# GpSimd scatters the results of a pair of expert blocks only once those of the pair ahead have landed

## The chip, the core and the metric

The kernel runs on one core of a Trainium2 chip. A core has five engines with instruction queues of their own: TensorE (PE, matmuls), VectorE (DVE), ScalarE (ACT), GpSimd (POOL) and SyncE (SP, which here only issues DMAs), and 16 DMA engines that serve all queues. The engines order their work by semaphores. The metric is the time of one execution on the device in microseconds (us), the median of several runs.

## What is computed

`x` has 8 sequences of 512 tokens with 128 channels. Each of the four layers adds to it something of its own layer norm: a time-mixing layer (RWKV), a mixture of experts, an attention with amplitude and phase, and the same mixture of experts again. The mixture of experts is what the change touches:

```python
logits = tokens @ router_w.T
topv, topi = jax.lax.top_k(logits, K)            # K = 2 of E = 8 experts
w = jax.nn.softmax(topv, axis=-1)
gate = jnp.zeros((T, n_experts)).at[jnp.arange(T)[:, None], topi].add(w)
for e in range(n_experts):
    h = jax.nn.gelu(tokens @ w1[e].T, approximate=False)
    y = h @ w2[e].T
    out = out + gate[:, e:e + 1] * y
```

There are 4096 tokens, `w1[e]` is 256 x 128 and `w2[e]` 128 x 256, all in float32.

## The kernel before, in words

The program is a row of stages with a barrier between them: mixing (`rwkv_phase`), experts (`moe_phase` with the names `moe0`), attention (`attention_stage`), experts again (`moe_phase`, `moe1`). Both calls of `moe_phase` run the same code.

A stage of experts has three parts.

1. *Sending.* For each of 8 batches of 512 tokens the norm, the router and the ranks are computed, and GpSimd scatters each token twice, once for each of its two experts, into `buffer` in DRAM (`send`, L1989). Every expert has a region there, and a row has 130 elements: the 128 channels, the number of the result's row (`ID`) and the gate (`GATE`).
2. *Blocks.* The rows are worked off in 72 blocks of 128 rows, two blocks to a unit, so 36 units (`BLOCKS`, `UNITS`). The expert of a block is read from a table that is made in the stage.
3. *Combining.* SyncE fetches the results of a batch, two rows for each token (L1842), and VectorE adds them to `x` (`add`, L2121 and L2123).

The order of part 2 is written out by hand on each engine, for unit i:

- SyncE loads block n into slot n % 16 of `blocked` (L1837). From block 16 on it waits first until the result of block n - 16 has been scattered and has landed, since the scatter reads its row numbers from that slot.
- TensorE runs in each step `turn_block(i+3)` (L1888, two transposes), `up(i+2)` (L1899), `turn_hidden(i+1)` (L1909, four transposes) and `down(i)` (L1919).
- ScalarE copies the turned block out of PSUM (`take_block`, L1962) and computes the gelu (L1968).
- VectorE copies the turned hidden rows (`take_hidden`, L2106) and multiplies the results by the gates into `weighed` (`weigh`, L2114). `weighed` has 8 slots (`HELD`), four units; `weigh` waits until the results that stood there four units ago have landed.
- GpSimd scatters a unit's two blocks of results, 128 rows of 512 bytes each, to their rows of `expert_results` in DRAM, with two indirect DMAs (`give_back`, L1996). It waits for `weighed_ready` alone. Each of the two DMAs adds 16 to the semaphore `returned[n % 8]` when it has landed.

So `returned[s]` has three kinds of reader before the change: `weigh` (four units behind), the loads of SyncE (eight units behind) and the start of part 3, where SyncE waits for all. The semaphores keep their counts from the first stage to the second (`returned_before`).

Of the kernel before, what the change touches and what calls it, by code (L numbers as in the profile page):

```python
# [15 lines left out]
P = 128  # L16
# [20 lines left out]
HELD = 8  # L37
# [1704 lines left out]
def moe_phase(nc, phase, rows, loads, norm, dispatch, following=None, output=None):  # L1742
# [11 lines left out]
    with ExitStack() as ctx:  # L1754
        def sb(name, shape, dt=F32):
            return ctx.enter_context(nc.sbuf_tensor(f"{phase}_{name}", shape, dt))
# [39 lines left out]
        hidden = sb("hidden", [P, 2, 2 * HT])  # L1796
        hiddenT = sb("hiddenT", [P, 2, 2 * HT])
        weighed = sb("weighed", [P, HELD, C])
        combined = sb("combined", [P, NB, TC, 2 * C])

        ps_x = [ps("ps_x0"), ps("ps_x1")]
# [9 lines left out]
        scattered, returned = dispatch.scattered, dispatch.returned  # L1811
        all_sent = [len(range(s, NB, 3)) * BATCH_SENT for s in range(3)]
        sent_before = [round_before * n for n in all_sent]
        returned_before = round_before * ALL_RETURNED
# [11 lines left out]
        @block.sync  # L1826
        def _(sp):
            sp.wait_ge(table_ready, 2)
            for s in range(3):
                sp.wait_ge(scattered[s], sent_before[s] + all_sent[s])  # L1830
            for n in range(BLOCKS):
                if n % AT_ONCE == 0:
                    rows_at = read_table(nc.sync, row_i, n, NE * REGION)
                if n >= SLOTS:
                    sp.wait_ge(returned[n % HELD], returned_before + 16 * ((n - SLOTS) // HELD + 1))
                at = rows_at[n % AT_ONCE]
                sp.dma_start(blocked[:, n % SLOTS, :], buffer[bass.ds(at, P), :]).then_inc(landed[n % SLOTS], 16)  # L1837
            for s in range(HELD):
                sp.wait_ge(returned[s], returned_before + ALL_RETURNED)
            for b in range(NB):  # L1840
                source = results[b * 2 * T:(b + 1) * 2 * T].rearrange("(t p k) c -> p t (k c)", p=P, k=2)
                sp.dma_start(combined[:, b], source).then_inc(fetched[b], 16)  # L1842
            if output is not None:
                for b in range(NB):
                    sp.wait_ge(added, b + 1)
                    batch = slice(b * T, (b + 1) * T)
                    sp.dma_start(output[0][:, batch], x[:, batch]).then_inc(output[1], 16)
                sp.wait_ge(output[1], 16 * NB)
# [133 lines left out]
        @block.gpsimd  # L1982
        def _(pool):
            def send(c):

                pool.wait_ge(indexed, c + 1)
                for t in range(TC):
                    for k in range(2):
                        pool.indirect_dma_start(buffer, bass.IndirectOffsetOnAxis(ap=index[:, c % 3, k, t:t + 1], axis=0),  # L1989
                                                sent[c % 3][:, t, k, :], None).then_inc(scattered[c % 3], 16)  # L1990

            def give_back(i):
                pool.wait_ge(weighed_ready, i + 1)
                for n in (2 * i, 2 * i + 1):
                    to = blocked[:, n % SLOTS, ID].bitcast(U32)
                    pool.indirect_dma_start(results, bass.IndirectOffsetOnAxis(ap=to, axis=0), weighed[:, n % HELD, :],  # L1996
                                            None, bounds_check=2 * REGION - 1, oob_is_err=False).then_inc(returned[n % HELD], 16)

            nc.gpsimd.memset(ones_b[:], 1.0)
            nc.gpsimd.memset(marks[:, TC, :], 0.0)  # L2000
            nc.gpsimd.memset(ones_row[:], 1.0).then_inc(prepared, 1)
            norm.on_pool(pool, 1)
            norm.on_pool(pool, 2)
            pool.wait_ge(prefilled[phase], 32)
            for c in range(NB):
                send(c)
                if c + 3 < NB:
                    norm.on_pool(pool, c + 3)
            for i in range(UNITS):
                give_back(i)  # L2010
            if following is not None:
                following.on_pool(pool, 0)
# [167 lines left out]
def program(nc, aps, out):  # L2180

    with ExitStack() as ctx:
# [4 lines left out]
        with ExitStack() as until_experts:  # L2187
            experts = Loaded(nc, until_experts, "experts_in", **EXPERT_SHAPES)
            first_norm = norm_of(nc, until_experts, "moe0", rows)
            first_norm.sent = [until_experts.enter_context(nc.sbuf_tensor(f"sent{s}", [P, TC, 2, ROW], F32))[:] for s in range(3)]  # L2190
            with ExitStack() as until_mixing:
                mixing = Loaded(nc, until_mixing, "mixing_in", w=[P, 1632], columns=[P, 10], sums=[P, 64 + 3 * P],
                                spread=[P, 4 * P])
                load_first(nc, aps, rows, mixing)
                rwkv_phase(nc, rows, mixing, first_norm,
                           lambda sp: load_rest(sp, aps, rows, experts, attention, dispatch))
            moe_phase(nc, "moe0", rows, experts, first_norm, dispatch, following=attention_norm)
# [5 lines left out]
                for tile, at in ((parts[0], 0), (parts[0], width), (parts[1], 0))]  # L2203
# [7 lines left out]
                        soft, value, parts, again, [aps[n] for n in EXPERT_SHAPES])  # L2211
        stored = ctx.enter_context(nc.semaphore("stored"))
        moe_phase(nc, "moe1", rows, again, last_norm, dispatch, output=(out, stored))


# [13 lines left out]
```

## Time and profile before

| | |
|---|---|
| median of 3 runs | 1271.28 us (1269.09 to 1277.58) |
| the profiled execution | 1281.76 us |
| its span, from the first to the last instruction | 1279.8 us |
| mean granted clock of TensorE in it | 0.83 of 2.4 GHz |
| blocks of the first stage of experts (first scatter of results to the first fetch) | 406.19 to 526.48 us |
| the same in the second stage | 1139.42 to 1260.01 us |

Times inside the kernel are those of the profiled execution, in us from the start of its span. A row of the timeline gives the start, the duration, the engine, the line and the tiles, the number of instructions put together, and in brackets how long the engine had been idle before and what ended that. "issue" stands for a wait on nothing that the profile shows, "remote" for an unknown releaser. The duration of an indirect DMA on GpSimd is that of the instruction, not of the transfer. The ends of TensorE's matmuls are modelled. SPq is the queue of SyncE.

### The profile page before, as it was taken

The page shows a single profiled execution, that of the slowest core. Times are in us where ns is not written, and L with a number is a line of the kernel's source. Part 1 is how long each engine was busy: PE and PEld are TensorE (multiplying, and loading weights), DVE is VectorE, ACT ScalarE, POOL GpSimd, SP SyncE. Part 2 cuts the span into 40 slices and gives each one's busy share as a digit, 9 for nine tenths or more (in the row PEclk, how much of TensorE's full clock was granted, in tenths as well). Part 3 has the DMA queues.
Part 4 walks back from the last instruction along what each step waited for, and adds up shares of the span by engine and source line. Part 5 has one row for each costly group of instructions (what it writes and reads, how often), then busy time and mean ns, then how long its engine had stood idle before and what let it go on. Part 6 is the DMA issues. An engine that isn't in the chain of part 4 may idle for free. (4 is left out here: it accounts for less than half of the span.)

```text
span 1279.8 us, 16765 instructions
## 1 busy us (share of the span) xinstructions
PE 916.4 (72%) x5108; PEld 568.8 (44%) x5108; DVE 786.1 (61%) x1787; ACT 503.2 (39%) x913; POOL 539.2 (42%) x578
## 2 busy tenths in 40 slices
PE   4889898974216788077789899989999832177780
PEld 1223322323215777034555566555666422056670
DVE  3878899876542233467777876886866365413334
ACT  1244444431002222077666666675655510022220
POOL 1455566535773556313113221231322267635552
PEclk9788899985557989578698998998999955578986
DMA  9999000000112222448787877887684011122226
GB/s 338 298 303 302 27 0 1 0 1 27 47 50 64 78 74 69 143 123 271 228 228 187 218 174 199 208 197 196 161 214 101 2 33 46 46 71 76 79 64 202
DMA packets 77585, 164.66 MB, mean 129 GB/s; under 512 B 14080, under 2 KB 42503, under 8 KB 75200
## 3 DMA queue, kind: packets, MB, share of 16 engines
q1 hardware_dynamic: 66752, 146.19, 41.7%
q0 software_dynamic: 8704, 16.93, 4.1%
q8 instruction: 42, 0.69, 0.2%
q10 hardware_dynamic: 2048, 0.53, 0.2%
q14 instruction: 39, 0.32, 0.1%
HBM read 107.63 MB, written 88.61 MB: 153 GB/s over the span
## 5 line engine op out<-in xcount | busy, mean ns | idle before, releaser
L1516 POOL TENSOR_SCALAR_AFFINE_SELECT attn_probs<-attn_probs 128x512 f32<-128x512 f32 x128 | 87.8, 720 | 291.2 <-ACT attn_probs L1345 291.2
L1996 POOL DMA_INDIRECT expert_results<-moe_weighed,moe_blocked x144 | 141.2, 981 | 129.5 <-DVE moe_weighed L2114 91.5
L1598 DVE TENSOR_REDUCE attn_maxima<-attn_ps_p 128x1 f32<-128x512 f32 (+3 forms) x235 | 145.9, 637 | 57.3 <-PE attn_ps_p L1092 53.0
L2106 DVE COPY moe_hiddenT<-moe_ps_h 128x512 f32<-128x512 f32 x72 | 49.6, 689 | 145.5 <-PE moe_ps_h L1909 123.0
L1087 PE MATMUL attn_ps_p<-attn_stack 96*128 96x384 f32 (+3 forms) x341 | 116.0, 383 | 7.8 <-DVE attn_maxima L1598 7.7
L670 POOL TENSOR_TENSOR rwkv_rs<-rwkv_recept,rwkv_state 128x512 f32<-128x512 f32 x64 | 76.0, 1187 | 106.8 <-DVE rwkv_state L752 106.8
L1135 PE MATMUL attn_ps_q<-attn_stack 128*128 128x128 f32 (+3 forms) x343 | 106.2, 373 | 2.6 <-DMA attn_stack<-attn_neg_max 1.8
L1598 DVE TENSOR_REDUCE attn_maxima<-attn_ps_t 128x1 f32<-128x384 f32 (+3 forms) x117 | 74.5, 637 | 35.6 <-PE attn_ps_t L1092 31.4
L752 DVE TENSOR_TENSOR_SCAN rwkv_state<-rwkv_decay,rwkv_kv 128x512 f32<-128x512 f32 x64 | 91.5, 1430 | 3.2
L1962 ACT COPY moe_blockT<-moe_ps_x 128x256 f32<-128x256 f32 x72 | 26.8, 373 | 158.2 <-PE moe_ps_x L1888 97.2
L1160 PE MATMUL attn_ps_o<-attn_probs,attn_v_ones 128*32 128x512 f32 (+3 forms) x1024 | 84.4, 449 | 0.6 <-POOL attn_probs L1516 0.6
L1087 PEld LDWEIGHTS attn_ps_p<-attn_stack 96*128 96x128 f32 x341 | 65.6, 205 | 18.4 <-DVE attn_maxima L1598 13.0
L1989 POOL DMA_INDIRECT moe_buffer<-parts,moe_index x64 | 61.8, 966 | 22.9 <-issue 18.8
L1989 POOL DMA_INDIRECT moe_buffer<-sent,moe_index x64 | 62.2, 972 | 20.9 <-issue 19.3
L1135 PEld LDWEIGHTS attn_ps_q<-attn_stack 128*128 128x128 f32 x343 | 59.9, 198 | 24.5 <-issue 13.5
L1968 ACT ACTIVATE moe_hidden<-moe_ps_u 128x512 f32<-128x512 f32 x72 | 43.1, 599 | 58.2 <-PE moe_ps_u L1899 40.4
L1087 PE MATMUL attn_ps_t<-attn_stack 96*128 96x512 f32 (+3 forms) x171 | 60.5, 387 | 5.8 <-DVE attn_maxima L1598 5.5
L419 PE MATMUL rwkv_ps_p<-rwkv_xf,mixing_in_w 128*128 128x512 f32 (+1 forms) x80 | 51.5, 730 | 17.5 <-POOL rwkv_xf L664 17.4
L1888 PE MATMUL moe_ps_x<-identity,moe_blocked 128*128 128x128 f32 x144 | 31.4, 298 | 44.6 <-DMA moe_blocked<-moe_buffer 44.3
L1340 ACT ACTIVATE attn_probs<-attn_ps_q 128x512 f32<-128x512 f32 x85 | 51.2, 602 | 25.7 <-PE attn_ps_q L1135 24.9
L1952 ACT COPY moe_xT<-moe_ps_x 128x512 f32<-128x512 f32 x16 | 9.4, 585 | 127.3 <-issue 76.9
L1135 PE MATMUL attn_ps_v<-attn_stack 128*128 128x512 f32 (+3 forms) x169 | 53.6, 379 | 7.8 <-DMA attn_stack<-attn_neg_max 4.4
(278 smaller groups left out, 2208.6 us busy)
## 6 DMA issues: line engine op xcount, KB each, us to landing
moe_buffer<-in_pad SPq DMA_DIRECT2D x2, 16640.0 KB, 88.3
attn_kept<-parts SPq DMA_DIRECT2D x32, 768.0 KB, 4.5
attn_stack<-attn_kept SPq DMA_DIRECT2D x128, 192.0 KB
attn_stack<-attn_kept SPq DMA_DIRECT2D x128, 96.0 KB
moe_blocked<-moe_buffer SPq DMA_DIRECT2D x144, 65.0 KB
value<-attn_values SPq DMA_DIRECT2D x35, 256.0 KB, 4.6
moe_combined<-expert_results SPq DMA_DIRECT2D x16, 512.0 KB
attn_values<-attn_early SPq DMA_DIRECT2D x2, 1792.0 KB, 5.7
```

Source lines behind the costliest of these rows:

```text
L419: mm(out[0:width, :], w[0:moving.shape[0], start:start + width], moving, start=True, stop=True).then_inc(prod_done, 1)
L670: tt(rs[:, n, :], recept[:, s, :], state[:, n, 0:T], ALU.mult).then_inc(rs_ready, 1)
L752: nc.vector.tensor_tensor_scan(state[:, n, 1:T + 1], decay[:, s, :], kv[:, n % 2, :], 0.0, ALU.mult, ALU.add).then_inc(state_ready, 1)
L1087: return mm(tiles(m)[:, i, :], stack[0][q][0:ROWS, h + i, t * P:(t + 1) * P], stack[1][q][0:ROWS, h + i, 0:(t + 1) * P], **flags)
L1135: return mm(ps_h[n % 3][:, at:at + width], stack[1][q][:, h, j * P:(j + 1) * P], stack[0][q][:, h, j * P:T], start=True, stop=True)
L1160: last = mm(ps_o[32 * hh:32 * hh + 32, j * P:T], v_ones[:, b % 2, j, 4 * g + hh, :], probs[:, g % 2, hh, at:at + width], start=(g % 2 == 0 ...
L1340: fn(out[:, h, 0:4 * P], ps_h[n % 3], ACT.Exp, scale=SCALE).then_inc(exp_done, 1)
L1516: nc.gpsimd.affine_select(out=tile, in_=tile, compare_op=ALU.is_ge, fill=0.0, base=0, pattern=[[0, 4], [1, P]], channel_multiplier=-1).the ...
L1598: nc.vector.tensor_reduce(maxima[:, u % 2, h:h + heads, t], tiles, AX_X, ALU.max).then_inc(g_free, 1)
L1989: pool.indirect_dma_start(buffer, bass.IndirectOffsetOnAxis(ap=index[:, c % 3, k, t:t + 1], axis=0), sent[c % 3][:, t, k, :], None).then_i ...
L1996: pool.indirect_dma_start(results, bass.IndirectOffsetOnAxis(ap=to, axis=0), weighed[:, n % HELD, :], None, bounds_check=2 * REGION - 1, o ...
L2106: nc.vector.tensor_copy(hiddenT[:, i % 2, :], ps_h[i % 2][:]).then_inc(hiddenT_ready, 1)
```

## The change

At the end of `give_back(i)` GpSimd waits until the second of the two scatters that it has just issued has landed. The next thing in its queue is the wait for the next unit's weighed results. A tile `pause` of 1 KB a partition is declared too, ahead of `combined`, and is neither written nor read.

```diff
@@ -1796,6 +1796,7 @@
         hidden = sb("hidden", [P, 2, 2 * HT])
         hiddenT = sb("hiddenT", [P, 2, 2 * HT])
         weighed = sb("weighed", [P, HELD, C])
+        pause = sb("pause", [P, 2 * P])
         combined = sb("combined", [P, NB, TC, 2 * C])
@@ -1995,6 +1996,7 @@
                     to = blocked[:, n % SLOTS, ID].bitcast(U32)
                     pool.indirect_dma_start(results, bass.IndirectOffsetOnAxis(ap=to, axis=0), weighed[:, n % HELD, :],
                                             None, bounds_check=2 * REGION - 1, oob_is_err=False).then_inc(returned[n % HELD], 16)
+                pool.wait_ge(returned[(2 * i + 1) % HELD], returned_before + 16 * ((2 * i + 1) // HELD + 1))
```

For i = 0 this is a wait for 16 on `returned[1]`, for i = 4 a wait for 32 on the same. No instruction changes its place on any engine.

## Rows read from the trace of the kernel before

**Rows 1.** The page: busy time of each engine (share of the span) and instructions.

```profile
PE 916.4 (72%) x5108; PEld 568.8 (44%) x5108; DVE 786.1 (61%) x1787; ACT 503.2 (39%) x913; POOL 539.2 (42%) x578
```

**Rows 2.** Stretches: busy time of each engine (instructions), granted clock, DMA share, GB/s.

```profile
404.00:519.00 115.00, 93.09 (x621) 82.89 (x619) 36.87 (x69) 30.30 (x66) 66.86 (x68) 0.93 0.26 71
1138.00:1253.00 115.00, 94.08 (x614) 82.42 (x612) 36.93 (x71) 30.17 (x65) 65.88 (x68) 0.94 0.26 70
463.00:469.00 6.00, 5.52 (x22) 5.08 (x23) 2.15 (x5) 1.63 (x4) 3.63 (x4) 0.50 0.25 66
```

**Rows 3.** Timeline of GpSimd, first stage, from the first scatter of results.

```profile
406.19 0.99 POOL L1996 DMA_INDIRECT expert_results<-moe_weighed,moe_blocked  x1 [17.22 <-DVE moe_weighed L2114]
407.49 0.99 POOL L1996 DMA_INDIRECT expert_results<-moe_weighed,moe_blocked  x1 [0.30 <-issue]
...
413.19 0.98 POOL L1996 DMA_INDIRECT expert_results<-moe_weighed,moe_blocked  x1 [2.13 <-DVE moe_weighed L2114]
414.48 0.98 POOL L1996 DMA_INDIRECT expert_results<-moe_weighed,moe_blocked  x1 [0.30 <-issue]
...
419.62 0.98 POOL L1996 DMA_INDIRECT expert_results<-moe_weighed,moe_blocked  x1 [0.30 <-issue]
423.09 0.98 POOL L1996 DMA_INDIRECT expert_results<-moe_weighed,moe_blocked  x1 [2.49 <-DVE moe_weighed L2114]
```

**Rows 4.** Timeline of GpSimd and SyncE: ends of the stages, and the second's first scatter.

```profile
524.26 0.98 POOL L1996 DMA_INDIRECT expert_results<-moe_weighed,moe_blocked  x1 [0.30 <-issue]
526.48 4.06 SPq L1842 DMA_DIRECT2D moe_combined<-expert_results  x6
...
1139.42 0.99 POOL L1996 DMA_INDIRECT expert_results<-moe_weighed,moe_blocked  x1 [15.09 <-DVE moe_weighed L2114]
...
1257.80 0.98 POOL L1996 DMA_INDIRECT expert_results<-moe_weighed,moe_blocked  x1 [0.31 <-issue]
1260.01 1.48 SPq L1842 DMA_DIRECT2D moe_combined<-expert_results  x3
```

**Rows 5.** Timeline of TensorE: one unit at full and one at half clock.

```profile
407.17 0.38 PE L1888 MATMUL moe_ps_x<-identity,moe_blocked 128*128 128x128 f32 x2
...
409.58 0.38 PE L1888 MATMUL moe_ps_x<-identity,moe_blocked 128*128 128x128 f32 x2
...
463.48 2.05 PE L1919 MATMUL moe_ps_y<-experts_in_w,moe_hiddenT 128*128 x8 [1.00 <-DVE moe_hiddenT L2106]
...
468.31 1.71 PE L1919 MATMUL moe_ps_y<-experts_in_w,moe_hiddenT 128*128 x8
```

**Rows 6.** Timeline of TensorE, ScalarE and VectorE, first stage.

```profile
416.35 1.06 PE L1919 MATMUL moe_ps_y<-experts_in_w,moe_hiddenT 128*128 x8
...
417.25 0.38 PE L1888 MATMUL moe_ps_x<-identity,moe_blocked 128*128 128x128 f32 x2
...
421.90 0.42 DVE L2114 TENSOR_TENSOR moe_weighed<-moe_ps_y,moe_blocked 128x256 f32<-128x256 f32 x1 [2.23 <-PE moe_ps_y L1919]
421.94 0.37 ACT L1962 COPY moe_blockT<-moe_ps_x 128x256 f32<-128x256 f32 x1 [5.23 <-PE moe_ps_x L1888]
```

**Rows 7.** Waits of 404 to 528 us: waiter and releaser, us in total, times, longest.

```profile
POOL expert_results L1996 <- DVE moe_weighed L2114: 47.4, 14, 17.2
...
ACT moe_blockT L1962 <- PE moe_ps_x L1888: 28.0, 14, 5.2
...
POOL expert_results L1996 <- issue: 18.1, 58, 0.7
```

**Rows 8.** Timeline of SyncE, first stage: the loads from block 16 on.

```profile
408.62 14.06 SPq L1837 DMA_DIRECT2D moe_blocked<-moe_buffer  x10
```

**Rows 9.** Timeline of VectorE, first stage: the first weighing.

```profile
404.96 0.43 DVE L2114 TENSOR_TENSOR moe_weighed<-moe_ps_y,moe_blocked 128x256 f32<-128x256 f32 x1 [0.20 <-PE moe_ps_y L1919]
```

## The prediction

> **What bounds the kernel now.** I read the page first. No engine is busy for more than 72% of the span, and GpSimd is at 42% [rows 1], so a wait on GpSimd costs nothing unless GpSimd ends last in the stage where it is put. The wait stands in `give_back`, which runs only in the two stages of expert blocks, so the next view is the table of stretches: 404 to 519 us and 1138 to 1253 us. There TensorE is busy for 93.1 and 94.1 us of 115, at a granted clock of 0.93 and 0.94, VectorE for 37, ScalarE for 30, and GpSimd for 66.9 and 65.9 us [rows 2].
>
> A busy share says little of GpSimd here, so the third view is its own timeline. A scatter is recorded with 0.98 us, but in a row of ready ones the next starts 1.29 us after the last (413.19 to 414.48 us) [rows 3]. A unit of two therefore takes 2.58 us of GpSimd, against a pace of one unit in 3.34 us: from the first scatter to the seen end of the last it is 526.48 - 406.19 = 120.3 us in the first stage and 1260.01 - 1139.42 = 120.6 us in the second [rows 4], and (120.3 - 3.5) / 35 = 3.34, where 3.5 is a last unit (1.29 + 2.2, below).
>
> What fills the rest? TensorE at full clock has a unit in 2.41 us (407.17 to 409.58) [rows 5]. The stage isn't at that pace, because VectorE and ScalarE act late in every third unit or so. TensorE's two L1888 matmuls start at 417.25 and run 0.38 us, and ScalarE's copy of them starts at 421.94, after 5.23 us of idle time; VectorE weighs at 421.90 what TensorE had from the L1919 group of 416.35 [rows 6]. GpSimd works without a pause from 413.19 until 420.60, and both are let go 1.3 us later [rows 3, 6]. So the stage goes in bursts: about three units of results in a row, six scatters, a pause of 2.1 to 2.5 us in which GpSimd waits for the next weighing. The table of waits has it: GpSimd waits 47.4 us for L2114 in 14 pieces, one of them the 17.2 us ahead of the first [rows 7]. GpSimd can wait 30.2 us in a stage, and loses nothing by a wait that falls into those. That is the slack against which the change must be set.
>
> Who could be holding them up? The rows show ScalarE, which is no partner of GpSimd in any of these instructions, idle for 5.23 us beside a row of scatters [rows 6]. The Trainium skill, SBUF — State Buffer, section "Who interferes with whom", has only VectorE and GpSimd share a port, and says that TensorE and ScalarE have their own. By it the bursts hold nobody up, and spacing them can return nothing; the trace does not agree with that. The sum below doesn't hang on it, since what TensorE could win is not what sets the new pace.
>
> **What the change does, and its price.** It adds one wait at the end of each `give_back(i)`, for the landing of block 2i+1, 36 in each stage and 72 in all; a tile that nothing reads is declared beside it (no instruction, no cost). No instruction moves to another place. What is queued behind the wait is the next unit's pair of scatters, and after the last unit of the first stage GpSimd's one small `pow` of the next norm, which waits for sums over fetched results that come later still, so nothing is lost there. SyncE waits for scatters that are 8 units back and VectorE for those 4 units back, and TensorE for VectorE.
>
> Before, GpSimd's two scatters of unit i+1 could start at once behind those of unit i. Now the chain of one unit is, on GpSimd alone:
> - From the first scatter's start to the second's: 1.29 us [rows 3].
> - From the second's start until a waiting queue has seen it land. Two rows give it: the last scatter of a stage starts at 524.26 and 1257.80, and SyncE, which waits for it, issues at 526.48 and 1260.01: 2.22 and 2.21 us [rows 4]. These end a row of eight. Scatter 0, alone after 17 us of rest, starts at 406.19, and SyncE's load that waits for it is issued at 408.62, 2.43 us [rows 3, 8]. A lone scatter is thus no faster. I take 2.2, and keep 2.43 as the upper end.
> - From there to the next unit's first scatter. GpSimd has to start anew from a wait, and its rows after a wait show what that takes: the weighing ends at 404.96 + 0.43 = 405.39 and the scatter starts at 406.19, 0.80 us; the one at 421.90 ends at 422.32 and the scatter starts at 423.09, 0.77 us [rows 3, 6, 9]. I take 0.79. Some 0.1 us of the 2.2 may be SyncE's own way from its wait to its issue; I leave it in, for the block loads that now land beside a scatter.
>
> Sum: 1.29 + 2.2 + 0.79 = 4.28 us for a unit. The work that GpSimd did in 2.58 us now takes 4.28 us, and 4.28 is above the 3.34 us at which the stage runs. The slack of 0.76 us a unit doesn't cover the 1.70 us that are added. A stage becomes 35 x 4.28 + 3.5 = 153.3 us long, which is 33.0 us more than 120.3 and 32.7 us more than 120.6; together +65.7 us. The profiled execution took 1281.8 us (span 1279.8), so it would be 1347.5. The median of the runs shown is 1271.3, 0.8% under it, and since the sum is made of waits I put the same microseconds on the median: 1271.3 + 65.7 = 1337.0 us.
>
> The Trainium skill, DMA: Bandwidth & Descriptors, section "Anatomy of one DMA — SWDGE (gpsimd) path", fits such a transfer with 2.0 us and its bytes over 436 GB/s. Estimated from that page, 64 KB are 2.15 us, the unit 4.23 us and the result 1333 us. The trace agrees within 0.1 us.
>
> **Bounds of each term.** The 1.29 us is the same in all rows of two scatters and isn't varied. The landing: 2.2 to 2.43; with 2.43 the unit is 4.51 and the time 1271.3 + 2 x (35 x 4.51 + 3.7) - 240.9 = 1353.5. The restart: 0.79 if all of it lies behind the wait, nothing if GpSimd prepares the next scatter while it waits; then the unit is 3.49 and the time 1271.3 + 2 x (35 x 3.49 + 3.5) - 240.9 = 1281.7. I am near the full 0.79, because the wait stands ahead of the scatter in one queue, as the wait for the weighing does now.
>
> What hides nothing: TensorE has 2.41 us of work a unit at full clock, so it is idle for 1.9 us of each 4.28. What if the clock goes? At a granted clock of 0.50 (the stretch from 463 us) [rows 2] a unit takes TensorE 4.83 us (463.48 to 468.31) [rows 5], more than 4.28. If TensorE were at 1.2 GHz all along, it would be the bound: 2 x (35 x 4.83 + 3.5) - 240.9 = +104.2, 1375.5 us. At a full clock for a part of the time it catches up 1.87 us a unit and loses 0.55 at half, with four units of room in `weighed`, so the clock would have to be at half for more than three quarters of the units (1.87 / 2.42) to be felt.
>
> **Rivals.**
> 1. The restart is hidden. The unit is 3.49 us, the time 1282, +0.8%: not slower by what can be told. For it: back to back, only 0.30 us separate two scatters [rows 3]. Against it: those have no wait between them, and every scatter behind a wait has some 0.8 us. It decides from a restart under 0.1 us; at a landing below 2.05 us besides it would be a gain.
> 2. The spacing frees TensorE's results and the landing is quicker when only one pair is in flight, so that GpSimd's pace falls under 3.34 us and the kernel is faster. At a unit of 3.1 us it is 1271.3 + 2 x (35 x 3.1 + 3.3) - 240.9 = 1254. For it: the late results of [rows 6] come only beside rows of scatters. Against it: the lone scatter with its 2.43 us.
> 3. TensorE's clock stays at half: 1375.5 us. For it: it is idle for 44% of each unit. Against it: in both stages it was granted 0.93 with waits of more than 2 us in them.
> 4. The wait is over before GpSimd comes to it, so nothing changes: 1271. It would need a landing within the 0.98 us of the instruction, which no row has.
>
> **Chances.** Forecast (a unit of 4.0 to 4.6 us): 0.82. Rival 1: 0.05, rival 2: 0.03, rival 3: 0.05, rival 4: 0.01, and 0.04 for a unit between 3.6 and 4.0 us. The forecast's own cases go from 4.0 us (1271.3 + 2 x 143.5 - 240.9 = 1317) to 4.6 (1359). The range takes in a little of the cases beside it at both ends: 1308 to 1365 us. About 1% is what a measurement of this kernel tells from no change. Slower by more takes the forecast, rival 3 and the cases between: 0.91; within 1%: rivals 1 and 4, 0.06; faster: rival 2, 0.03.
>
> **What would show it.** In the profile of the changed kernel GpSimd's scatters should stand in pairs, 1.29 us inside the pair and 4.28 from pair to pair, with some 3.0 us between the start of the second and the start of the next pair; a pair's restart should follow a landing and not L2114. The stage should last 153 us, twice. TensorE should show one wait a unit of about 1.9 us in place of the bursts, and its releaser should be the weighing. The forecast is wrong if the pairs stand closer than 3.6 us, if the stages keep their bursts, or if TensorE's unit is at 4.8 us with a granted clock near 0.50.

## The result

| | median | range | runs |
|---|---|---|---|
| before | 1270.2 us | 1266.1 to 1277.6 | 4 |
| changed | 1355.6 us | 1347.4 to 1359.5 | 4 |

The ratio is 1.0657, with a 95% interval of 1.0587 to 1.0727: slower by 75 to 92 us. The forecast was 1337 us with a range of 1308 to 1365. The profiled execution took 1359.5 us (span 1357.7), 77.7 us more than that of before.

The page of the changed kernel, busy time of each engine:

```profile
PE 941.6 (69%) x5108; PEld 580.1 (43%) x5108; DVE 788.9 (58%) x1787; ACT 506.8 (37%) x913; POOL 541.0 (40%) x578
```

These stand against [rows 1]: GpSimd is busy for 541.0 us as against 539.2, VectorE and ScalarE for 3 to 4 us more, and TensorE for 25 us more, at a lower granted clock. Of the longer stages nearly all is idle time. The timeline of GpSimd in the first stage of experts, which answers to [rows 3]:

```profile
419.61 0.98 POOL L1997 DMA_INDIRECT expert_results<-moe_weighed,moe_blocked  x1 [2.04 <-DMA expert_results<-moe_weighed,moe_blocked]
420.89 0.98 POOL L1997 DMA_INDIRECT expert_results<-moe_weighed,moe_blocked  x1 [0.30 <-issue]
423.91 0.98 POOL L1997 DMA_INDIRECT expert_results<-moe_weighed,moe_blocked  x1 [2.03 <-DMA expert_results<-moe_weighed,moe_blocked]
425.20 0.98 POOL L1997 DMA_INDIRECT expert_results<-moe_weighed,moe_blocked  x1 [0.31 <-issue]
```

The rows of up to eight scatters are gone. There are pairs, 1.29 us inside the pair and 4.30 from pair to pair (419.61 to 423.91), and what ends the 2.03 us of idle time before a pair is the landing of the last scatter, no longer the weighing. The ends of the stages answer to [rows 4]; the first scatters are at 410.98 and 1179.14 us:

```profile
566.52 0.98 POOL L1997 DMA_INDIRECT expert_results<-moe_weighed,moe_blocked  x1 [0.30 <-issue]
...
568.74 7.00 SPq L1843 DMA_DIRECT2D moe_combined<-expert_results  x8
...
1335.56 0.98 POOL L1997 DMA_INDIRECT expert_results<-moe_weighed,moe_blocked  x1 [0.30 <-issue]
1337.77 0.93 SPq L1843 DMA_DIRECT2D moe_combined<-expert_results  x2
```

The stages last 568.74 - 410.98 = 157.8 and 1337.77 - 1179.14 = 158.6 us, 75.5 us more together than before. That is nearly all of the 77.7 us by which the two profiled executions differ. The table of waits of 404 to 560 us, against [rows 7]:

```profile
POOL expert_results L1997 <- DMA expert_results<-moe_weighed,moe_blocked: 66.0, 31, 4.3
PE moe_ps_x L1889 <- DMA moe_blocked<-moe_buffer: 28.6, 36, 1.8
...
POOL expert_results L1997 <- DVE moe_weighed L2116: 18.2, 2, 16.2
```

GpSimd waited 47.4 us for L2114, and has 18.2 us left of it (16.2 of them ahead of the first scatter); in its place stand 66.0 us of landings. New is that TensorE waits for the loads of blocks, 36 times and 28.6 us.

### The profile page after: what moved, and what is told of

The parts are those of the page before. It is cut to its first block and busy times, and to the rows that moved or that the text cites. A ratio compares the mean times of both kernels' runs of the same rounds, so it can differ in the third digit from the quotient of the medians.

```text
span 1357.7 us, 16837 instructions
## 1 busy us (share of the span) xinstructions
PE 941.6 (69%) x5108; PEld 580.1 (43%) x5108; DVE 788.9 (58%) x1787; ACT 506.8 (37%) x913; POOL 541.0 (40%) x578
## 5 line engine op out<-in xcount | busy, mean ns | idle before, releaser
L1889 PE MATMUL moe_ps_x<-identity,moe_blocked 128*128 128x128 f32 x144 | 42.4, 324 | 107.9 <-DMA moe_blocked<-moe_buffer 107.4
L1889 PEld LDWEIGHTS moe_ps_x<-identity,moe_blocked 128*128 128x128 f32 x144 | 21.1, 151 | 124.5 <-issue 73.7
L1087 PEld LDWEIGHTS attn_ps_p<-attn_stack 96*128 96x128 f32 x341 | 66.3, 207 | 18.6 <-DVE attn_maxima L1598 12.9
L664 POOL TENSOR_TENSOR rwkv_xf<-rwkv_mixed,rwkv_xT 128x512 f32<-128x512 f32 x40 | 51.7, 1293 | 18.1 <-DVE rwkv_mixed L717 16.0
```

Of the source, the lines that this page charges most:

```text
L664: tt(xf[:, (f + s) % 2, :], mixed[:, (f + s) % 2, :], xT[:, 1:T + 1], ALU.add).then_inc(xf_ready, 1)
L1087: return mm(tiles(m)[:, i, :], stack[0][q][0:ROWS, h + i, t * P:(t + 1) * P], stack[1][q][0:ROWS, h + i, 0:(t + 1) * P], **flags)
L1889: last = nc.tensor.transpose(ps_x[i % 2][:, q * P:(q + 1) * P], blocked[:, n % SLOTS, 0:C], ident[:])
```

## The experiments

The runs were taken in four groups, each on one chip together with the kernel before, and a ratio is always to the kernel before of the same group: experiments 1 to 4 (the record numbers the chip 0), 5 to 8 (again 0), 9 and 10 (2), 11 and 12 (14). The expectations say "call" for such a group. "Unit" below is the time from one pair's first scatter to the next pair's, read from the trace of each run; "stage" runs from the first scatter of results to the first fetch.

**1. The tile without the wait**

```diff
-                pool.wait_ge(returned[(2 * i + 1) % HELD], ...)
```

> The change without its wait: only the unused tile is declared, which moves the tile behind it by 1 KB a partition. Theory 1 (all of the lost time is the wait): as before, about 1270 us, a ratio of 1.00, stages of 120 us. Rival (the 12 to 20 us by which the change cost more than the 65.7 us forecast come from the moved tile, not from the wait): slower by 12 to 20 us, 1282 to 1290.

Measured: 1278.7 us beside 1277.9, ratio 0.9997 (0.9958 to 1.0035), stages of 117.5 and 118.3 us. The moved tile costs nothing that can be told; the lost time is the wait's.

**2. A wait for the unit ahead**

```diff
-                pool.wait_ge(returned[(2 * i + 1) % HELD], returned_before + 16 * ((2 * i + 1) // HELD + 1))
+                if i >= 1:
+                    pool.wait_ge(returned[(2 * i - 1) % HELD], returned_before + 16 * ((2 * i - 1) // HELD + 1))
```

> The wait stays, once a unit, but for the landing of the unit ahead: 72 waits less 2, each over before it is reached (the earlier unit's second scatter lands 2.2 us after its start, GpSimd is done with the next two only 2.57 us after it). Theory 1 (the cost is the landing and the restart laid open behind it, 4.30 us a unit): nothing is laid open, the stages stay at 120 to 122 us, 1270 us. Rival (a wait on GpSimd between two scatters costs by itself, because GpSimd then no longer prepares the next one): the pace of two scatters in a row goes from 2.57 to 2.57 + 0.5 = 3.1 us or more, still under 3.34, and the bursts get shorter; the time between 1265 and 1290.

Measured: 1276.2 us beside 1277.9, ratio 0.9992 (0.9963 to 1.0021); stages of 118.7 and 121.8 us, units of 2.57 us in the rows, as before. A wait that is already over costs GpSimd nothing. It is the laid-open landing that costs, and one unit of distance hides it.

**3. and 4. A slot for every block, without and with the wait**

```diff
-    SLOTS = 16
+    SLOTS, LANDINGS = BLOCKS, 16
...
-        landed = [sem(f"landed{s}") for s in range(SLOTS)]
+        landed = [sem(f"landed{s}") for s in range(LANDINGS)]
...
-                if n >= SLOTS:
-                    sp.wait_ge(returned[n % HELD], returned_before + 16 * ((n - SLOTS) // HELD + 1))
+                if n >= LANDINGS:
+                    sp.wait_ge(landed[n % LANDINGS], 16 * (n // LANDINGS))
```

> The kernel before, without the wait, with 72 slots for blocks in place of 16, so that SyncE's loads wait for no landing of results, only for the load 16 blocks ahead; all loads are issued in the first third of the stage. Theory A on the bursts of the kernel before (results of TensorE are seen late when SyncE issues a load while GpSimd is in a row of scatters): bursts in the first third only, from there a unit in 2.6 us (GpSimd's two scatters), stages of about 100 us, 1230 us. Theory B (a row of scatters by itself holds the results up): the bursts stay over the whole stage, 120 us, 1270 us. It says besides whether the ring of 16 slots set the pace before.

> 72 slots and the wait of the change. Theory 1: GpSimd's chain of 4.30 us a unit is the bound and doesn't know of the slots, so 1350 us as the changed kernel, stages of 154 to 158 us. Rival 2 (what the change cost beyond the forecast, 12 to 20 us, is TensorE's wait for blocks, 28.6 us in the first stage of the changed kernel, since the loads are released by later landings): without the ring the units at 4.6 to 6.5 us go, stages of 152 to 153.5 us, 10 us under the changed kernel, 1340 us or less.

Measured without the wait: 1279.1 us beside 1277.9, ratio 1.001 (0.9971 to 1.005), stages of 119.0 and 119.1 us. The loads of the first stage are over before 450 us. From there to 524 us the DMA table of the stage knows scatters and a few instruction packets only:

```profile
q0 software_dynamic: 1497, 2.77, 11.2%
q8 instruction: 4, 0.07, 0.4%
q14 instruction: 2, 0.02, 0.1%
...
expert_results<-moe_weighed,moe_blocked POOLq DMA_INDIRECT x47
```

and the bursts are still there, as the timeline of the same kernel shows at 452 to 457 us:

```profile
453.55 0.98 POOL L1996 DMA_INDIRECT expert_results<-moe_weighed,moe_blocked  x1 [0.30 <-issue]
...
455.85 0.42 DVE L2114 TENSOR_TENSOR moe_weighed<-moe_ps_y,moe_blocked 128x256 f32<-128x256 f32 x1 [2.23 <-PE moe_ps_y L1919]
455.89 0.37 ACT L1962 COPY moe_blockT<-moe_ps_x 128x256 f32<-128x256 f32 x1 [3.83 <-PE moe_ps_x L1888]
...
457.04 0.98 POOL L1996 DMA_INDIRECT expert_results<-moe_weighed,moe_blocked  x1 [2.52 <-DVE moe_weighed L2114]
```

The last scatter of the row ends at 454.53 us, and 1.3 to 1.4 us later VectorE's weighing and ScalarE's copy of turned rows start, the copy after 3.83 us of idle time. My theory A (it takes SyncE's issues besides) is refuted, theory B (a row of scatters suffices) stands. Nor was the ring of 16 slots what set the pace.

Measured with the wait: 1358.1 us, ratio 1.0658 (1.0586 to 1.0731), stages of 158.7 and 159.5 us. It is the changed kernel's time to 0.2%, without the ring that TensorE waits on there (and without the unused tile). So TensorE's 28.6 us for blocks are no cause: it has run ahead as far as the slots let it, and waits where GpSimd's chain makes it wait. The equal time hides one difference. SyncE issues its loads until 438.07 us here, and the first seven units of the stage, which fall into that time, take 4.45 to 5.25 us, 2.4 us more in all than at 4.30. What rules TensorE out by itself is the table of waits of the changed kernel: ahead of GpSimd's scatters 31 waits end with a landing and only two with a weighing, one of them that of the first scatter.

**5. A wait behind each scatter**

```diff
                                             None, ...).then_inc(returned[n % HELD], 16)
+                    pool.wait_ge(returned[n % HELD], returned_before + 16 * (n // HELD + 1))
-                pool.wait_ge(returned[(2 * i + 1) % HELD], ...)
```

> A wait for the landing behind every scatter, 144 in all. Theory 1 (each laid-open landing costs 2.2 us and each restart 0.79 from the start of a scatter): 2 x (2.23 + 0.79) = 6.02 us a unit in the median, stages of 35 x 6.02 + 5.2 = 216 us plus what late landings add, together about 1271 + 2 x (216 to 223) - 241 = 1462 to 1476 us. A rival in which the wait costs something only because the results of the next unit are late (TensorE starved) would not double the addition of a unit and stays under 5.3 us, 1410 us. On the landings that come 1 to 2 us late in the changed kernel (4 to 5 in each stage): if it is instruction packets of 16 KB on the same DMA engines, more of them fall into a landing here, as GpSimd is waiting for one more of its time: 5 to 8 units in each stage beyond 6.3 us.

Measured: 1473.4 us (2 runs), ratio 1.2089 (1.2 to 1.2178); unit 6.02 us in the median, stages of 218.5 and 218.9 us. The timeline of GpSimd:

```profile
418.75 0.98 POOL L1997 DMA_INDIRECT expert_results<-moe_weighed,moe_blocked  x1 [2.04 <-DMA expert_results<-moe_weighed,moe_blocked]
421.76 0.98 POOL L1997 DMA_INDIRECT expert_results<-moe_weighed,moe_blocked  x1 [2.03 <-DMA expert_results<-moe_weighed,moe_blocked]
424.80 0.98 POOL L1997 DMA_INDIRECT expert_results<-moe_weighed,moe_blocked  x1 [2.05 <-DMA expert_results<-moe_weighed,moe_blocked]
```

One scatter from start to start is 3.01 us where a landing and a restart lie behind it, as my two rows had made it (2.2 + 0.79). The second part of the expectation missed: 3 units in each stage are beyond 6.3 us, not 5 to 8.

In this group the kernel before took 1220.5 us (13 runs, 1212.7 to 1226.4), not 1270 to 1280. It holds for experiments 5 to 8, which are of one group; experiment 9 takes it up.

**6. A wait behind every second unit**

```diff
-                pool.wait_ge(returned[(2 * i + 1) % HELD], ...)
+                if i % 2 == 1:
+                    pool.wait_ge(returned[(2 * i + 1) % HELD], ...)
```

> The wait only behind every second unit: rows of four scatters. Theory 1: two units take 3 x 1.29 + 2.2 + 0.79 = 6.88 us, 3.44 a unit, if nothing else holds GpSimd; stages of 35 x 3.44 + 3.5 = 124 us plus some late landings, 1277 to 1290 us. Theory C (results of TensorE are seen late only once GpSimd has been in a row of scatters for some 3.5 us): rows of 5.2 us still hold some results up, but with four units of room it isn't felt. Rival (the bursts stay and the wait is added to them): 3.34 + 0.85 = 4.2 us a unit, 1330 us.

Measured: 1278.2 us beside 1220.5, ratio 1.0502 (1.0426 to 1.0578); units of 2.57 and 4.3 us in turn, 3.47 in the mean, for 3.44 by the sum. The chain's arithmetic holds. On theory C it says nothing, as no bursts were there in this group.

**7. and 8. Another break: GpSimd fills the unused tile**

```diff
# 7: and waits for its own fill
+                nc.gpsimd.memset(pause[:], 0.0).then_inc(paused, 1)
+                pool.wait_ge(paused, i + 1)
# 8: and waits only for the fill of the unit ahead
+                if i >= 1:
+                    pool.wait_ge(paused, i)
+                nc.gpsimd.memset(pause[:], 0.0).then_inc(paused, 1)
```

> In place of the wait for the landing, GpSimd fills the unused tile (128x256) and waits for its own fill. Theory 1: the landing goes out of the unit and the restart stays: 2.57 + fill 0.3 to 0.5 + restart 0.5 to 0.8 = 3.4 to 3.9 us a unit in place of 4.30, stages of 122 to 140 us, 1275 to 1310 us. Theory C: the short break in each unit is enough for the results of TensorE to get through, so the bursts go. Rival (only a landing, with no transfer in flight, lets them through): the bursts stay, and the unit is longer than the sum above.

> The same fill behind each unit, but GpSimd waits only for the fill of the unit ahead, long over. It separates GpSimd's queue standing still from its cores doing something other than scatters. If a queue that stands still is what lets TensorE's results through, the bursts stay here, 3.34 us a unit or a little more: 1271 to 1285 us. If any other work between the scatters is enough, the unit is 2.57 + 0.3 to 0.5 = 2.9 to 3.1 us without bursts, stages of 105 to 112 us, 1240 to 1255 us, which would be faster than both kernels.

Measured: 7 took 1273.7 us beside 1220.5, ratio 1.0431 (1.0356 to 1.0507), unit 3.37 us, a little under the 3.4 to 3.9 that I had expected. Its timeline shows the restart without a landing:

```profile
412.72 0.98 POOL L1997 DMA_INDIRECT expert_results<-moe_weighed,moe_blocked  x1 [0.30 <-issue]
413.68 0.35 POOL L1999 MEMSET moe_pause<- 128x256 f32 x1
414.80 0.98 POOL L1997 DMA_INDIRECT expert_results<-moe_weighed,moe_blocked  x1 [0.77 <-POOL moe_pause L1999]
```

The fill ends at 413.68 + 0.35 = 414.03 us, and the scatter starts at 414.80: 0.77 us, the term that I had put at 0.79. 8 took 1230.5 us, ratio 1.0095 (1.0056 to 1.0134), unit 2.76 us, no bursts. Both of my expectations for it missed, since a fill adds 0.19 us to a unit and not 0.3 to 0.5. Taken alone the time looks like 1270 turned into 1230 by a fill of 0.35 us; beside the 1220.5 us of the same group it is 10 us lost.

**9. and 10. The kernel before itself, and the fill once more**

> The kernel before, unchanged, to have its own profile beside the others: it took 1278 us in the first call of experiments and 1220 us in the second. 57 us is what the bursts come to: two stages of 35 units at 3.34 in place of 2.57 us are 54 us. Theory D (whether TensorE's results are held up beside a row of scatters differs from chip to chip, or from time to time on one, and not by kernel): either the time is 1270 to 1280 with units of 2.57 and 4.4 to 5.4 us mixed, or it is 1215 to 1225 with 2.57 us throughout, stages of 93 to 95 us, and nothing else in the trace differs. Rival (the faster time comes from another stage, by the clock of TensorE): the stages of experts stay at 120 us, and another stage is 50 us shorter.

> The fill behind each unit once more (it waits only for the fill of the unit ahead), beside the kernel before on the same chip. It was 1230.5 us beside 1220.5. If this call finds the kernel before at 1270 to 1280 us: by theory E (the fill lets TensorE's results through, so the bursts go) 1225 to 1235 us, a ratio of 0.96; by theory D (the fill does nothing to the bursts, which were away in that call) 1275 to 1285, a ratio of 1.00 to 1.01. If it finds it at 1220 us: 1230 us, 70 x 0.19 us more, by both.

Measured: the unchanged kernel 1221.0 us beside 1219.6, the fill 1232.3, ratio 1.0094 (1.0057 to 1.0131). The profile of the unchanged kernel in this group has a span of 1216.8 us, 63.0 less than the 1279.8 of the profile before. First its timeline on GpSimd, ScalarE and VectorE:

```profile
414.01 0.98 POOL L1996 DMA_INDIRECT expert_results<-moe_weighed,moe_blocked  x1 [0.30 <-issue]
...
415.30 0.98 POOL L1996 DMA_INDIRECT expert_results<-moe_weighed,moe_blocked  x1 [0.30 <-DVE moe_weighed L2114]
...
416.58 0.98 POOL L1996 DMA_INDIRECT expert_results<-moe_weighed,moe_blocked  x1 [0.30 <-issue]
...
416.74 0.38 PE L1888 MATMUL moe_ps_x<-identity,moe_blocked 128*128 128x128 f32 x2
...
416.94 0.42 DVE L2114 TENSOR_TENSOR moe_weighed<-moe_ps_y,moe_blocked 128x256 f32<-128x256 f32 x1 [0.20 <-PE moe_ps_y L1919]
...
417.16 0.37 ACT L1962 COPY moe_blockT<-moe_ps_x 128x256 f32<-128x256 f32 x1 [0.95 <-PE moe_ps_x L1888]
```

then stretches of it, two of experts, one of mixing and one of attention:

```profile
404.00:490.00 86.00, 81.15 (x602) 75.26 (x600) 38.34 (x69) 30.77 (x64) 65.57 (x68) 0.99 0.33 92
1104.00:1190.00 86.00, 81.30 (x601) 75.17 (x600) 38.26 (x69) 30.72 (x64) 65.56 (x68) 1.00 0.34 94
0.00:300.00 300.00, 246.36 (x711) 88.29 (x711) 238.03 (x386) 111.35 (x174) 142.96 (x127) 0.89 0.42 135
500.00:940.00 440.00, 374.65 (x2482) 238.18 (x2486) 334.18 (x645) 284.18 (x511) 104.19 (x142) 0.91 0.77 202
```

and the last two of before for comparison:

```profile
0.00:300.00 300.00, 245.67 (x711) 87.70 (x711) 238.86 (x394) 111.35 (x174) 143.53 (x128) 0.89 0.43 135
530.00:970.00 440.00, 375.82 (x2470) 238.41 (x2470) 332.87 (x643) 283.64 (x510) 104.18 (x142) 0.91 0.77 201
```

The instructions and the program are the same, mixing and attention have nearly the same busy times in a stretch of the same length, and the stages of experts last 93.7 and 93.3 us in place of 120.3 and 120.6. That is 53.9 of the 63.0 us. Unit after unit takes 2.57 us, and ScalarE's copy starts 0.04 us after the turned group (416.74 + 0.38) in place of 4.3 us [rows 6]. Theory D holds: whether results of TensorE are held up beside a row of scatters differs from group to group with the same kernel, and the rival by another stage or the clock doesn't (the late copy of [rows 6] falls into 416 to 424 us, where the granted clock is 1.00).

The traces say more, by the times at which they have the semaphores updated. In the kernel before with bursts TensorE's groups that end at 416.51, 417.41 and 417.63 us have their updates at 418.95, 421.87 and 421.92 us, and those of its next four groups follow by 422.17. They come in order, the first of them in the middle of the row of scatters and the other six in a heap, 1.3 us behind its end (420.60 us). So ScalarE and VectorE don't see a signal late; the signal itself comes late, while TensorE goes on to its next groups (417.46 and 418.33 us). Of the 241 updates by TensorE that the trace has for the two stages 99 are over 1 us late; of VectorE's none is, nor any by TensorE in the profile of experiment 9. And the two kinds of group differ in one thing besides: in all eight profiles of kernels run with bursts about, the changed kernel's two among them, at least 5 to 8% of the updates by instructions are missing (217 of 3492 in the kernel before), all from the two stretches in which GpSimd scatters (301 to 524 and 1034 to 1258 us there); in the six profiles of the other two groups all are there. A lateness and a loss of records come together, then. Whether both have one cause, and whether the recording has a part in the lateness, is open: every execution on record has a recorded span. Nor does a run tell whether it is the chip; the record has number 0 for a group of either kind, which speaks against it if that is one chip.

**11. and 12. The change and the fill in one more call**

> The changed kernel, unchanged, beside whatever the kernel before does in this call. Theory 1 (GpSimd's own chain of 4.30 us a unit is the bound, and it doesn't know of the bursts): 1345 to 1360 us in either case, stages of 157 to 160 us; the ratio is 1.065 if the kernel before has its bursts (1270 to 1280 us), and 1.11 if it has none (1215 to 1225 us), as 70 x (4.42 - 2.57) = 130 us. Rival (what took the bursts away in the last two calls makes landings quicker too): stages under 150 us, 1335 us or less.

> The fill behind each unit, waiting only for the fill of the unit ahead. With the kernel before at 1270 to 1280 us in this call: theory E (any break in the row of scatters lets TensorE's results through) 1225 to 1235 us, a ratio of 0.96, units of 2.76 us; theory D (it does nothing to the bursts) 1275 to 1290, units of 2.76 mixed with such of 4 us and more. With the kernel before at 1220 us: 1230 us, and the question stays open.

Measured: the kernel before took 1279.0 us here, so the bursts were there again. The changed kernel took 1358.5, ratio 1.0666 (1.0583 to 1.0748), stages of 158.2 and 158.8 us, unit 4.30. The fill took 1276.3 us, ratio 0.9993 (0.9959 to 1.0027). Its timeline of GpSimd:

```profile
414.19 0.98 POOL L1997 DMA_INDIRECT expert_results<-moe_weighed,moe_blocked  x1 [0.17 <-issue]
415.47 0.98 POOL L1997 DMA_INDIRECT expert_results<-moe_weighed,moe_blocked  x1 [0.30 <-issue]
416.42 0.36 POOL L2001 MEMSET moe_pause<- 128x256 f32 x1
416.95 0.98 POOL L1997 DMA_INDIRECT expert_results<-moe_weighed,moe_blocked  x1 [0.16 <-issue]
418.24 0.98 POOL L1997 DMA_INDIRECT expert_results<-moe_weighed,moe_blocked  x1 [0.30 <-issue]
419.19 0.35 POOL L2001 MEMSET moe_pause<- 128x256 f32 x1
421.38 0.98 POOL L1997 DMA_INDIRECT expert_results<-moe_weighed,moe_blocked  x1 [1.84 <-DVE moe_weighed L2118]
```

Units of 2.76 us stand beside such of 4.43 (416.95 to 421.38): the bursts are whole, theory E falls, and the 1230 us of experiments 8 and 10 were those of groups without bursts. The fill costs 10 us there and nothing here, since here it fills a part of the time in which GpSimd had to wait anyway. No version of these beats the kernel before: those with a laid-open wait are slower; of the others the fill costs 1% without bursts, and all are the same as the kernel before with them.

## Why the prediction was right, and where it was short

*The bound.* The forecast rested on GpSimd's own chain, and that is what the trace shows: median unit 4.30 us for 4.28, in both stages, in the first result and in experiments 4 and 11, with 16 slots or 72. The parts were shown one by one: the pair at 1.29 us, landing and restart together at 3.01 (experiment 5), the restart alone at 0.77 (experiment 7), a satisfied wait at nothing (experiment 2).

*The sum.* It gave 153.3 us a stage; the measured ones are 157.8 and 158.6. Of the 4.5 and 5.3 us, 0.7 are the 0.02 us a unit. The rest is a term that I had no case for, single late units, most of them with a late landing: 4 units of the first stage and 5 of the second took 4.6 to 6.5 us. The landing was put at 2.2 to 2.43 us for all of them. (One reading of the rows was wrong without harm: the last scatter of the first stage ends a row of four, not of eight.) The timeline of GpSimd around the latest of the second stage, and the DMA table of 1194 to 1198 us:

```profile
1192.50 0.98 POOL L1997 DMA_INDIRECT expert_results<-moe_weighed,moe_blocked  x1 [2.05 <-DMA expert_results<-moe_weighed,moe_blocked]
1193.78 0.98 POOL L1997 DMA_INDIRECT expert_results<-moe_weighed,moe_blocked  x1 [0.30 <-issue]
1198.52 0.98 POOL L1997 DMA_INDIRECT expert_results<-moe_weighed,moe_blocked  x1 [3.76 <-DMA expert_results<-moe_weighed,moe_blocked]
```

```profile
q8 instruction: 1, 0.02, 1.7%
...
moe_blocked<-moe_buffer SPq DMA_DIRECT2D x2, 65.0 KB, 3.0
expert_results<-moe_weighed,moe_blocked POOLq DMA_INDIRECT x1, 4.0
```

One DMA packet of an engine's instructions, 16 KB and 1.1 us on its DMA engine, is in this stretch, and the scatter took 4.0 us to land in place of 2.2. In both profiles of the changed kernel (the first and that of experiment 11) 24 such packets fall into the stages. The 12 that begin 2.2 to 3.1 us after a unit's first scatter, shortly before or while the second one's data and its count are moved (2.7 to 3.3 us), have units of 5.1 to 6.5 us; of the other 12, eleven have 4.29 to 4.31 us and one 4.75, which a weighing ends. Before, GpSimd hadn't to wait for any of this. That the packet delays the landing is read from this coincidence; no run removed the packets. In experiment 5, which waits for more landings, late units were fewer than I expected, so how much a packet costs isn't settled. Three late units come at the same places in both profiles of the changed kernel (unit 8 of the first stage, 4.64 us, and unit 24 of both stages, 4.8 to 5.3 us, where the second scatter follows after 1.75 us), and I have no cause for them that was tested.

*Own time and median.* The two stages hold 75.5 us of the 77.7 between the profiled executions, where the forecast had 65.7; the 9.8 us of difference are the late units and the 0.02 us of above. The medians of the result differ by 85.4 us, those of experiments 4 and 11 by 80.1 and 79.5 us, and the 25 runs of before beside experiments 1 to 4 go from 1269 to 1290 us, so the last 5 to 8 us are no finding. With 1355.6 us the result lies 18.6 us over the forecast and 9 under the range's end; the range held it by its width, not because it had a case for late landings.

*What hides it.* The slack of 0.76 us a unit that I set against the 1.70 us was right for that group, but it is no property of the kernel. It comes from bursts that other groups don't have: at a unit of 2.57 us there is no slack. Experiment 6, with one landing for two units, shows it: 1278 us, as much as the kernel before in a group with bursts, and 58 us more than the kernel before of its own group. The changed kernel wasn't run in a group without bursts. As its chain doesn't know of them, about 1.11 would be the ratio there; that is an estimate from 1357 and 1220 us.

*TensorE.* Right was that the bursts go: in the changed kernel, on a chip where the kernel before has them, ScalarE's copy follows the turned group at once. The same view at 425 us:

```profile
425.20 0.98 POOL L1997 DMA_INDIRECT expert_results<-moe_weighed,moe_blocked  x1 [0.31 <-issue]
...
425.39 0.33 PE L1889 MATMUL moe_ps_x<-identity,moe_blocked 128*128 128x128 f32 x1 [0.35 <-DMA moe_blocked<-moe_buffer]
...
425.75 0.37 ACT L1963 COPY moe_blockT<-moe_ps_x 128x256 f32<-128x256 f32 x1 [2.26 <-PE moe_ps_x L1889]
...
428.15 0.98 POOL L1997 DMA_INDIRECT expert_results<-moe_weighed,moe_blocked  x1 [1.97 <-DMA expert_results<-moe_weighed,moe_blocked]
```

The group ends at 425.39 + 0.33 = 425.72 and the copy starts at 425.75 us. None of the 231 updates by TensorE that this trace has for the two stages is more than 0.1 us late. So pairs that are spaced by a landing hold nothing up, where a row of scatters with fills between them still does. The prediction set ScalarE's idle time in [rows 6] against what the Trainium skill says of shared ports. That was no test of it: ScalarE waited for TensorE's signal, and its copy starts 0.02 us after the late update of 421.92 us. Wrong was the releaser that I named: TensorE waits for the loads of blocks, not for the weighing, since with 8 units of slots and 3 of its own steps ahead it meets the end of the slots first. It didn't fall to 4.83 us a unit. The stretches of both stages, against [rows 2], have its granted clock at 0.89 and 0.88, with three tenths of the time idle:

```profile
404.00:560.00 156.00, 107.55 (x641) 91.11 (x639) 40.08 (x72) 34.06 (x70) 66.90 (x68) 0.89 0.20 54
1172.00:1330.00 158.00, 109.10 (x642) 91.90 (x640) 40.10 (x72) 34.07 (x70) 66.57 (x68) 0.88 0.20 54
```

*The rivals.* Rivals 1 and 4 fall with the 2.03 us of idle time before each pair (with the restart hidden it would be 1.2, with the wait over 0.3). Rival 2, a quicker landing of a lone pair, falls too: from the last scatter of the stages (566.52 and 1335.56) to SyncE's fetch it is 2.22 and 2.21 us, as before. Rival 3 falls with the clock.

## What to carry to other kernels

A wait for the landing of one's own DMA puts the whole landing and the restart between two DMAs, 3.0 us here where 1.29 stood, unless as much work stands between issue and wait; one unit of distance made it free. The price is set by the waiting queue's chain and not by its busy share, so write the chain down and compare it with the pace of the stage. And take the pace of a stage from more than one execution: the slack that a wait seems to fall into may be a disturbance that is away the next time.

## What was unexpected of the hardware

- The same program took 1278 us in one group of runs and 1220 in the next, each within 2% over 10 and more runs, with all but some 9 us of the difference in the two stages in which GpSimd scatters without a pause. In the slower case TensorE's updates of semaphores come up to 5.3 us late (experiment 3) and in a heap, mostly 1 to 2 us after the row of scatters has ended, while VectorE's are on time; and some of the updates are missing from the trace. It takes no other DMA of the kernel beside the scatters (experiment 3), it isn't changed by other work of 0.35 us between them (experiment 12) nor by a wait that is over (experiment 2), and it is away if each pair is followed by some 2 us of rest (the change). A row ends when the next results are missing, so the order of events alone doesn't tell which holds which; that spacing the pairs takes the lateness away does. A rest between 0.3 and 2.0 us wasn't run in a group with bursts, apart from the fill.
- Single packets of 16 KB of instructions coincide with scatters that land 0.8 to 2.2 us late.
